# Audio tower kernel: the mask rows are broadcast from SBUF instead of through DRAM, one head step is reordered, and the third score product gets another PSUM bank

## The reference, cut to what matters

```python
def reference(x, W, b, sim, gates, q_proj, k_proj, v_proj, o_proj):   # 16 batches
    h = gelu(x[:, 1:] @ W[:256] + x[:, :1] @ W[256:] + b)             # 374 tokens
    y = layernorm(h)                                                  # attention 1
    cos = (y @ y.T) / max(|y_i| |y_j|, 1e-8)
    h = h + softmax(cos) @ y + y
    z = layernorm(h)                                                  # 8 experts, d = 128
    logits = (z/|z|) @ (sim/|sim|) - sigmoid(gates)
    mask = logits > 0            # where a token has none: its top 2 experts
    route = softmax over the chosen experts of relu(logits)
    q, k, v = [sum_e mask[t, e] * (z[t] @ proj[e]) for proj in (q_proj, k_proj, v_proj)]
    a = softmax(causal(q @ k.T / sqrt(128))) @ v                      # attention 2
    return h + z + sum_e mask * route[t, e] * (a[t] @ o_proj[e])
```

## Time and profile before

| what | value |
|---|---|
| median of 3 runs | 699.05 us (698.8 to 699.39) |
| the profiled execution, its own time | 699.35 us |
| its span, first to last instruction | 697.6 us |
| mean granted TensorE clock | 0.998 |
| busy: PE, DVE, POOL, ACT | 681.4, 546.7, 405.8, 345.4 us |
| DMA: bytes, mean rate | 57.29 MB, 82 GB/s |
| mask_all<-d_mask, issue to landing, median of 32 | 4.3 us |

### The profile page before, as it was taken

The page is one execution under the profiler, slowest core; times in us unless marked ns, Lnnn a source line. Parts: engine busy times, 40 slices in busy tenths (PEclk is TensorE's granted clock), DMA queues, the critical chain, the costliest instruction groups (busy, mean ns, idle before and its releaser), DMA issues.

```text
span 697.6 us, 17459 instructions
## 1 busy us (share of the span) xinstructions
PE 681.4 (98%) x4856; PEld 435.9 (62%) x4856; DVE 546.7 (78%) x1428; ACT 345.4 (50%) x768; POOL 405.8 (58%) x669
## 2 busy tenths in 40 slices
PE   9999989999999999999999999999999999999998
PEld 8887656565655656565655656565655656565555
DVE  5778868786979788796979788796979788786636
ACT  5977444444536354444636354444636354453443
POOL 7552325665747676565747676565747676563534
PEclk9999999999999999999999999999999999999999
DMA  9671142424324252423334242423334242422121
GB/s 247 161 183 50 62 103 43 107 53 90 69 50 112 49 117 49 103 54 87 67 53 112 49 117 46 106 54 86 66 55 112 49 117 45 107 57 68 24 75 31
DMA packets 128310, 57.29 MB, mean 82 GB/s; under 512 B 100264, under 2 KB 124056, under 8 KB 128152
## 3 DMA queue, kind: packets, MB, share of 16 engines
q1 hardware_dynamic: 127888, 56.60, 35.0%
q10 hardware_dynamic: 392, 0.32, 0.1%
HBM read 30.45 MB, written 9.01 MB: 57 GB/s over the span
## 4 chain that ended last, share of the span: by engine, by line
PE 81%; DVE 6%; issue 5%; POOL 3%; DMA 2%; ACT 2%; DVEq 0%; POOLq 0%; ACTq 0%; SPq 0%
PE bank L1820 70%; PE bank L1884 2%; PE bank L1888 2%; PE bank L1886 2%; DVE xm L1407 2%; PE bank L1740 2%; PE bank L1729 1%; DMA mask_all<-d_mask 1%; DMA xT<-xhl 1%; DVE region_b L1290 1%; DMA region_b<-in_x_dram 1%; DVE exp_hl L1428 1%; DVE region_a L1488 1%; POOL small L660 0%; DVE xinT L1211 0%
## 5 line engine op out<-in xcount | busy, mean ns | idle before, releaser
L1820 PE MATMUL bank<-xm,w_qkv 128*128 128x374 f16 x2304 | 409.6, 323 | 0.0
L1820 PEld LDWEIGHTS bank<-xm,w_qkv 128*128 128x128 f16 x2304 | 223.4, 98 | 146.8 <-issue 0.6
L1033 ACT ACTIVATE region_c<-bank,out_w 128x256 f32<-128x256 f32 x180 | 83.3, 473 | 159.1 <-PE bank L1820 142.4
L1820 PE MATMUL bank<-w_o,aoT 128*128 128x512 f16 x540 | 143.1, 379 | 0.4
L1407 DVE TENSOR_TENSOR xm<-xT,mask_all 128x1496 f16<-128x1496 f16 x128 | 139.5, 1103 | 1.5 <-DMA mask_all<-d_mask 1.3
L1312 DVE SCALAR_TENSOR_TENSOR h<-bank,out_w,h 128x256 f32 (+1 forms) x180 | 85.9, 477 | 47.5 <-ACT region_c L1033 45.2
L748 POOL TENSOR_TENSOR region_c<-region_c 128x512 f32<-128x512 f32 x46 | 68.7, 1493 | 25.4 <-ACT region_c L1033 20.5
L787 POOL TENSOR_TENSOR exp_hl<-exp,exp_hl 128x128 f16<-128x128 f32 (+2 forms) x48 | 50.5, 1053 | 56.4 <-ACT exp_hl L976 54.3
L1820 PEld LDWEIGHTS bank<-w_o,aoT 128*128 128x128 f16 x540 | 49.2, 98 | 51.4 <-DVE h L1312 12.9
L755 POOL TENSOR_TENSOR region_c<-region_c 128x256 f32<-128x256 f32 x46 | 47.6, 1034 | 5.8 <-POOL region_c L748 5.5
L902 ACT ACTIVATE aoT<-bank 128x374 f16<-128x374 f32 x15 | 7.2, 483 | 87.7 <-PE bank L1820 87.7
(11 more groups left out here) (211 smaller groups left out, 1026.1 us busy)
## 6 DMA issues: line engine op xcount, KB each, us to landing
mask_all<-d_mask SPq DMA_DIRECT2D x32, 384.0 KB, 4.3
h<-in_x_dram SPq DMA_DIRECT2D x16, 256.0 KB, 4.9
out_dram<-h SPq DMA_DIRECT2D x31, 128.0 KB
rnorm_row<-d_rnorm SPq DMA_DIRECT2D x16, 192.0 KB, 3.6
d_v<-xinT SPq DMA_DIRECT2D x14, 192.0 KB, 4.4
xinT<-d_v SPq DMA_DIRECT2D x56, 48.0 KB, 2.3
h<-in_x_dram SPq DMA_DIRECT2D x15, 112.0 KB, 5.6
out_dram<-h SPq DMA_DIRECT2D x15, 112.0 KB
```

Of the source, the lines that this page charges most:

```text
L1033: a.activation(prod[:, prod_buf(n, t), q, :], pair_bank(n, p)[:, C:2 * C], ACT.Copy, scale=weights_out(n)[:, t, 2 * q + 1:2 * q + 2]).then ...
L1820: last = t_.matmul(dst, left[lp], right[rp], start=(starts and k == 0), stop=(stops and k == 2), skip_group_check=True)
```

## The change

The mask no longer goes through DRAM: SP issues eight DMAs, one for each expert, and each reads one partition of maskT and writes it to all 128 partitions of mask_all. Each half's semaphore now counts four transfers, and ScalarE waits for all of them before it writes maskT again. In the head's last step, batch 2's norm is applied right behind the routing on VectorE, its high part comes ahead of the turned mask on ScalarE, its low part ahead of the routing weights on POOL, and SP transposes its rows ahead of loading the norms. In the branch with f and n, the third score goes to `turn[0]` and no longer waits for the first score's evacuation.

```diff
--- before.py
+++ after.py
@@ -164,7 +164,6 @@
         d_rnorm = nc.dram_tensor("d_rnorm", [B, TP], F32, kind="Internal").ap()
         d_route = nc.dram_tensor("d_route", [(NT - 1) * E * P], F32, kind="Internal").ap()
         d_v = nc.dram_tensor("d_v", [B, P * TP], F32, kind="Internal").ap()
-        d_mask = nc.dram_tensor("d_mask", [B, E * TP], F16, kind="Internal").ap()
 
 
         bank = [ctx.enter_context(nc.psum_tensor(f"bank{i}", [P, 512], F32)) for i in range(8)]
@@ -264,7 +263,6 @@
         s_route_exp = sem("route_exp")
         s_mask_turned = sem("mask_turned")
         s_mask_row = sem("mask_row")
-        s_mask_stored = sem("mask_stored")
         s_mask_loaded = [sem("mask_loaded0"), sem("mask_loaded1")]
         s_xm_ready = sem("xm_ready")
         s_q_done = sem("q_done")
@@ -464,14 +462,11 @@
             def mask_around(f):
 
                 sp.wait_ge(s_mask_row, f + 1).then_inc(s_passed, 1)
-                sp.dma_start(d_mask[f, :].rearrange("(e t) -> e t", e=E), maskT[:, :]).then_inc(s_mask_stored, 16)
-                sp.wait_ge(s_mask_stored, 16 * (f + 1)).then_inc(s_passed, 1)
                 if later(f):
                     sp.wait_ge(s_xm_ready, E * f).then_inc(s_passed, 1)
-                for k in range(2):
-                    sp.dma_start(mask_all[:, k * (E // 2):(k + 1) * (E // 2), :].rearrange("p e t -> p (e t)"),
-                                 d_mask[f, k * (E // 2) * TP:(k + 1) * (E // 2) * TP].partition_broadcast(P)).then_inc(
-                                     s_mask_loaded[k], 16)
+                for e in range(E):
+                    sp.dma_start(mask_all[:, e, :], maskT[e:e + 1, :].unsqueeze(1).broadcast_to([1, P, TP])).then_inc(
+                        s_mask_loaded[e // (E // 2)], 16)
 
             def values_out(m):
 
@@ -584,12 +579,14 @@
                     second_rows_around(f)
                 if g is not None:
                     norms_out(g)
+                    if early(m):
+                        first_rows_around(g)
                     norms_in(g)
                 if f is not None and not early(m):
                     mask_around(f)
                 if m is not None and by_trip(m):
                     values_out(m)
-                if g is not None:
+                if g is not None and not early(m):
                     first_rows_around(g)
                 if m is not None and by_trip(m):
                     values_in(m)
@@ -797,10 +794,10 @@
                 if g1 is not None:
                     norm_rows(0, g1, 1.0, 1e-38)
                     row_scales(g1)
+                if early(m):
+                    low_1(g1)
                 if f is not None:
                     route_weights(f)
-                if early(m):
-                    low_1(g1)
                 if final(n):
                     pool.wait_ge(s_tile_summed, 2 * NT * n).then_inc(s_passed, 1)
                     sum_products(n, 0)
@@ -949,7 +946,8 @@
             def turned_mask(f):
                 act.wait_ge(s_mask_turned, f + 1)
                 if later(f):
-                    act.wait_ge(s_mask_stored, 16 * f)
+                    for s in s_mask_loaded:
+                        act.wait_ge(s, 16 * (E // 2) * f)
                 a.activation(maskT[:, :], as16(turn[1] if later(f) else turn[0], TP)[0:E, :], ACT.Copy).then_inc(s_mask_row, 1)
 
             def route_exp(f):
@@ -1047,10 +1045,10 @@
                     weights_high(2 * NC)
                     weights_high(2 * NC + 1)
                     head_high(qT, qkv_bank[0], s_q_done, m + 1, s_q_hi, [], qkv_out)
+                    high_1(g1)
                     turned_mask(f)
                     route_exp(f)
                     values_out(m)
-                    high_1(g1)
                     output_weights_high(0)
                     output_weights_high(1)
                     high_k()
@@ -1397,7 +1395,7 @@
             def mask_tokens(b, e):
 
                 if e % (E // 2) == 0:
-                    dve.wait_ge(s_mask_loaded[e // (E // 2)], 16 * (b + 1))
+                    dve.wait_ge(s_mask_loaded[e // (E // 2)], 16 * (E // 2) * (b + 1))
                 if e == 0:
                     second_rows_turned(dve, b)
                 if later(b):
@@ -1536,13 +1534,13 @@
                     v.memset(v_out[:, T:TP], 0.0)
                     norm_stats(0, g1)
                     route(f)
+                    norm_apply(0, g1)
                     weights_low(2 * NC)
                     head_low(qT, qkv_bank[0], s_q_hi, m + 1, s_q_lo, qkv_out)
                     weights_low(2 * NC + 1)
                     weight_max(f)
                     weight_sum(f)
                     turn_values(m)
-                    norm_apply(0, g1)
                     for e in range(E - 4):
                         mask_tokens(f, e)
                         if e in (1, 3):
@@ -1561,7 +1559,7 @@
                     mask_scores(n, 1, out_bank[1])
                     exp_low(f, 2)
                     exp_lower(f)
-                    mask_scores(n, 2, out_bank[0])
+                    mask_scores(n, 2, turn[0])
                     mask_tokens(m, E - 2)
                     mask_tokens(m, E - 1)
                     residual(f)
@@ -1908,15 +1906,15 @@
                     last = t_.transpose(as16(turn[1] if later(f) else turn[0], TP)[:, t * P:(t + 1) * P], mask16[:, t, :], ident16[:, :])
                 last.then_inc(s_mask_turned, 1)
 
-            def score(n, i):
+            def score(n, i, banks=out_bank + out_bank[:1]):
                 if i == 0:
                     pe.wait_ge(s_q_lo, n + 1)
                     pe.wait_ge(s_k_lo, n + 1)
                     if later(n):
                         pe.wait_ge(s_pair_added, PAIRS * n)
-                if i == 2:
+                if i == 2 and banks[2] is banks[0]:
                     pe.wait_ge(s_scores_out, NT * n + 1)
-                split_product(out_bank[i % 2][:, 0:KEYS[i]], [qT[:, p, i * P:(i + 1) * P] for p in range(2)],
+                split_product(banks[i][:, 0:KEYS[i]], [qT[:, p, i * P:(i + 1) * P] for p in range(2)],
                               [kT[:, p, 0:KEYS[i]] for p in range(2)], True, True, s_scores_done)
 
             def last_scores(n):
@@ -2048,7 +2046,7 @@
                     score(n, 1)
                     M(4)
                     turn_exp(f)
-                    score(n, 2)
+                    score(n, 2, out_bank + [turn[0]])
                     M(5)
                     for t in range(NT):
                         attend(f, t)
```

## The result

The changed kernel takes 1062.9 us (median of 4 runs, 1061.5 to 1068.4) against 699.2 us for the kernel before (median of 4 runs, 698.8 to 700.8): the ratio is 1.521, 95% interval 1.515 to 1.527. The forecast was 689.8 us. The kernel takes half as long again, and the first rival, with "about 1000 us", is what happened.

A forecast was written before the change was run, and what follows sets the result against it. PE, busy 681.4 of 697.6 us, was taken as the bound, so only its waits and slow clock could yield. 3.9 + 4.9 + 0.5 = 9.3 us off 699.35 gives 690.05, as median 689.8 us; range 687.5 to 698.

The forecast's parts named there:

- the first rival: Mask reads: one source partition is a bottleneck, 3.5 us a row, some 310 us lost, about 1000 us; chance 0.20.
- the mask's way in the loop: Mask broadcast from SBUF in each loop pass: a row takes 0.5 us, about SP's issue spacing, so all is hidden.
- SP's pace: SP's issues of the eight mask transfers: 0.48 us each, taken from the spacing of the two loads.
- the head's own slow stretch: Head, behind PE's wait for batch 2's transposes: granted clock 0.60 from 100 to 102 us, costing 1.51 us.
- The break-even: Loop: time a mask row may take before the change's gains are lost, 0.9 us, or 0.8 with the values' store between.
- The slack of 0.73 us: Loop: time between the first rows' transposes landing and PE wanting them at 335.53, 0.73 us.
- The head's step: Head, batch 2's rows transposed sooner: PE's 2.42 us wait and 1.51 us of slow clock go, gaining 3.9 us.
- The third score: Loop, own bank for this score: 0.55 us wait becomes 0.17 at attend, gaining 13 x 0.38 = 4.9 us.
- The tail's 0.5 us: Tail, i = 15: without the store the mask lands before VectorE asks, gaining 0.5 us, with 0 as low bound.

The follow-up runs named there:

- everything but the mask: The changed kernel with the mask's old way through DRAM (store, wait, two loads), the rest of the change kept: 691.4 us, ratio 0.9888.
- the run with 16 partitions: The changed kernel, each of the eight transfers reading 16 neighbouring partitions of a constant tile, eight copies of each, real mask left out: 742.8 us, ratio 1.063.
- the run with eight rows from DRAM: The changed kernel with maskT stored to DRAM again and eight loads of one row each from there: 701.4 us, ratio 1.004.
- the run with 128 partitions: The changed kernel, each of the eight transfers copying a constant tile of 128 SBUF partitions, real mask left out: 691.4 us, ratio 0.9905.

## Why the prediction was wrong

**The step that failed** is that of the mask's way in the loop: "I take 0.5 us, which hides it all". A row takes 3.6 us. The bounds were right (the upper one, 3.5 us, was worked out), the choice between them was not. It went by the nearest rows in destination and shape, 197 to 446 GB/s, but these rows have another source, DRAM. The argument against the rival, that DRAM too serves all copies from one place, doesn't carry over: the rate of a source in SBUF follows the groups of four partitions it touches, 27 GB/s from one, 94 from four, and no limit seen from eight and more up to SP's pace, 150 GB/s. The chance of 0.20 was too low for a resource that no row showed.

**The size of the rival.** It had 310 us on top of the forecast: 21.6 us in each of 13 steps and 30 beside them. Against the run with everything but the mask, PE's waits are 312.8 - 2.4 = 310.4 us longer, so the sum is right. Its path is not quite: it had one wait for the transposes, where PE waits 122.8 / 14 = 8.8 us for VectorE and 163.8 / 14 = 11.7 us for them. Its rate, 27.9 GB/s, came out as well, but by luck in part. It took the rate for that of one DMA engine, the peak divided by 16, while the trace has the 16 engines 0.77 busy on average at 27 GB/s. What it left out is the clock: PE's busy time is 60.4 us longer, for which the head's own slow stretch was the warning.

**The break-even** of 0.8 to 0.9 us a row was too generous. At 0.88 us the run with 16 partitions lost 44 us to the kernel before. The forecast asked only when the queue is free. But the values' store is held back too (0.82 us instead of 0.35), and the transposes land 1.1 us later behind it. The slack of 0.73 us held. In the run with eight rows from DRAM the transposes went out 0.74 us later and landed after 4.3 us instead of 3.8 (medians). 0.74 + 0.5 - 0.73 = 0.5 us, and the waits were 7.1 / 14 = 0.5 us a step.

**SP's pace.** The spacing of 0.48 us came from two loads from DRAM; from SBUF it is 0.63 us where nothing holds SP back. With a fast source this size did no harm, as the run with 128 partitions shows.

**The head's step**: right, 3.4 of 3.9 us, with the wait gone and the clock at 1.00. **The third score**: right in mechanism, 4.5 of 4.9 us, with 12 new waits of 0.17 us where about 13 were forecast. Both together give 7.6 us of 8.8. **The tail's 0.5 us** was not seen by itself: with the slow mask it can't show, and no run has only the missing store.

The best version is that with the mask through DRAM and the rest of the change, 691.4 us, 1.1% faster than before. No run issues the mask from SBUF behind the transposes or from an engine other than SP. So it stays open how much of the loss comes from SP being held back and how much from the queue itself.

## What to carry to other kernels

Before a broadcast is moved from DRAM to SBUF, count the groups of partitions that its source touches. One partition feeds 16 DMA engines no faster than 27 GB/s; spread the source over many partitions first, or leave it in DRAM. Here a mask spread over 16 partitions a row was 4.5 us slower than the one from DRAM. An unknown rate is judged by rows with the same source, and the queue behind it sets the price: list what the same engine issues next, because a late transpose stops TensorE and then its clock falls too.

## What the runs showed of the hardware that was not expected

- The DMA engines show as 0.77 busy while they deliver 27 GB/s. A busy share says nothing of the rate.
- SP stands in a single issue for 3.1 us in the median, 4.0 at most: slow transfers hold back the engine that issues them, not only their queue.
- Transfers of one group each ran only about two at a time: two alternating groups gave 48 to 60 GB/s and took 12.8 us for eight issues, eight different groups 11.3 us. A transfer that touches four groups itself did not show this limit (94 GB/s).
